# Three low-row matrix products of a fused graph-attention and expert kernel, given 128 rows

## The reference, cut to what matters

```python
x = x + L0_gnn(layernorm(x), adj)   # h = xn @ W; f1 = h @ a1; f2 = h @ a2
                                    # e = leaky_relu(f1[:, None] + f2[None, :], 0.2)
                                    # a = softmax(where(adj > 0, e, -9e15), axis=1); elu(a @ h)
x = x + L0_ffn(layernorm(x))        # 8 experts, top 2, gelu
x = x + L1_gnn(layernorm(x), adj)   # attention whose scores depend on the kind of edge
x = x + L1_ffn(layernorm(x))        # 8 experts, each weighed by one softmax w of shape (1024, 8)
```

## Time and profile before

| | |
|---|---|
| median of 3 executions | 1168.76 us (1166.08 to 1174.06) |
| the profiled execution's own time | 1170.39 us |
| its span, first to last instruction | 1168.6 us |
| mean granted TensorE clock | 0.982 of full speed |
| first attention | 0 to 317 us |
| expert stage | 317 to 489 us |
| second attention | 489 to 813 us |
| last stage | 813 us to the end |

### The profile page before, as it was taken

How to read it: one execution, slowest core, us unless ns; L and a number is a source line. 1 busy time by engine, 2 the same in 40 slices (tenths; PEclk the granted TensorE clock), 3 DMA queues, 4 the chain that set the end, 5 groups by cost and what they waited for, 6 DMA issues and landing times. The chain is left out here.

```text
span 1168.6 us, 18925 instructions
## 1 busy us (share of the span) xinstructions
PE 1100.7 (94%) x5993; PEld 725.8 (62%) x5993; DVE 704.9 (60%) x2210; ACT 744.0 (64%) x1074; POOL 415.9 (36%) x475
## 2 busy tenths in 40 slices
PE   2998899899999999689999999998999999999998
PEld 2554445444477777557777777776546666666667
DVE  4779888888663436287888888864443333333335
ACT  2887777788665554366777777775666556565561
POOL 5327677866765222344556565211000000000000
PEclk9999899899999999899999999999999999999999
DMA  8977557655227665412222222110000000000001
GB/s 260 343 292 265 183 214 285 254 207 210 75 89 245 186 195 168 131 44 84 84 82 82 80 84 80 56 54 1 1 1 10 19 10 10 19 10 19 10 10 37
DMA packets 69142, 131.08 MB, mean 112 GB/s; under 512 B 9918, under 2 KB 30764, under 8 KB 68012
## 3 DMA queue, kind: packets, MB, share of 16 engines
q1 hardware_dynamic: 60268, 111.96, 28.5%
q0 software_dynamic: 8192, 16.79, 4.7%
q10 hardware_dynamic: 576, 1.05, 0.3%
HBM read 77.60 MB, written 52.17 MB: 111 GB/s over the span
## 5 line engine op out<-in xcount | busy, mean ns | idle before, releaser
L2227 PEld LDWEIGHTS eY<-Vo,dGW 128*128 128x128 f32 x1024 | 132.4, 191 | 54.0 <-issue 52.8
L507 POOL DMA_INDIRECT sorted_x<-V,AT_I x128 | 125.9, 984 | 55.8 <-issue 36.2
L2210 PE MATMUL eU<-XTN,V 128*128 128x512 f32 x256 | 132.9, 602 | 2.5 <-PEq L2145 2.5
L2227 PE MATMUL eY<-Vo,dGW 128*128 128x128 f32 x1024 | 134.2, 276 | 0.1
L673 PE MATMUL O<-Y,HS 128*128 128x512 f32 x256 | 134.0, 644 | 0.0
L1863 POOL DMA_INDIRECT W<-sorted_y,ROW_I x96 | 101.0, 1052 | 90.5 <-PE f_T L1923 71.7
L2218 PE MATMUL eU<-H,V 128*128 128x512 f32 x256 | 131.4, 595 | 0.0
L2397 DVE TENSOR_TENSOR dGW<-H,WBC 128x512 f32<-128x512 f32 x80 | 55.2, 691 | 125.2 <-PE eY L2227 125.0
L1942 PEld LDWEIGHTS f_O<-f_XN,f_PT 128*128 128x128 f32 x896 | 107.8, 192 | 25.3 <-issue 20.7
L2306 ACT ACTIVATE H<-eU,bn 128x512 f32<-128x512 f32 x128 | 99.5, 777 | 30.4 <-PE eU L2210 21.3
L1995 ACT COPY f_PT<-f_TP 128x512 f32<-128x512 f32 x128 | 68.7, 589 | 73.2 <-PE f_TP L1932 73.2
(11 more groups left out here) (305 smaller groups left out, 2034.2 us busy)
## 6 DMA issues: line engine op xcount, KB each, us to landing
XTN<-in_adj SPq DMA_DIRECT2D x64, 512.0 KB, 4.7
masks<-NMW SPq DMA_DIRECT2D x8, 2048.0 KB
f_MK<-masks SPq DMA_DIRECT2D x60, 256.0 KB, 2.7
sorted_y<-zero SPq DMA_DIRECT2D x39, 256.0 KB, 10.1
NMW<-sorted_x SPq DMA_DIRECT2D x39, 256.0 KB, 2.7
sorted_y<-NMW SPq DMA_DIRECT2D x39, 256.0 KB, 2.5
X<-in_x SPq DMA_DIRECT2D x8, 512.0 KB, 7.7
out_x<-X SPq DMA_DIRECT2D x16, 256.0 KB, 2.3
```

The source lines that it names most:

```text
L507: g_.indirect_dma_start(sorted_x, bass.IndirectOffsetOnAxis(ap=AT_I[b % 2][:, kt:kt + 1], axis=0), XR[b % 2][:, t * P:(t + 1) * P], None). ...
L2210: pe.matmul(U1[j % 2][:, :], V1[:, e * P:(e + 1) * P], XTN[:, b * N + q * HALF:b * N + (q + 1) * HALF], start=True, stop=True).then_inc(u1 ...
L2227: i = pe.matmul(Y[q][:, t * P:(t + 1) * P], GW[:, j % 2, t * P:(t + 1) * P], Vo[:, e * P:(e + 1) * P], start=(e == 0 and t == 0), stop=(e ...
```

## The change

Every product of few rows becomes one of 128 rows, and its result stays what it was:

- `ones` becomes one 128-row tile of ones for the whole program. POOL's second fill of such a tile goes.
- `F1R` has 128 rows. DVE zeroes it once at the start; the copy still writes three rows.
- `one_row` has 128 rows of 1/128, so the sum over 128 rows is again 1.0.
- `pick` and `WT3` have 128 rows. `pick` is zeroed in all of them, its pattern is written in 24; DVE zeroes `WT3` at the start of the last stage.

```diff
-        ones3 = sb("ones3", [3, P], BF16)
-        pick = sb("pick", [3 * E, E * P], BF16)
+        ones = sb("ones", [P, P], BF16)
+        pick = sb("pick", [P, E * P], BF16)
...
-                v = pick[:, :].rearrange("r (e m) -> r e m", e=E)
+                v = pick[0:3 * E, :].rearrange("r (e m) -> r e m", e=E)
...
-            one_row = tile("one_row", [1, HALF], BF16)
+            one_row = tile("one_row", [P, HALF], BF16)
-            F1R = tile("F1R", [3, 2, N], BF16)
+            F1R = tile("F1R", [P, 2, N], BF16)
-            before, ones = tile("before", [P, P], BF16), tile("ones", [P, P], BF16)
+            before = tile("before", [P, P], BF16)
...
-                op(g_.memset, ones[:, :], 1.0)
...
-                        i = pe.matmul(t[:, h * HALF:(h + 1) * HALF], ones3[:, :], F1R[:, b % 2, h * HALF:(h + 1) * HALF],
+                        i = pe.matmul(t[:, h * HALF:(h + 1) * HALF], ones[:, :], F1R[:, b % 2, h * HALF:(h + 1) * HALF],
...
-                            pe.matmul(O[:, h * HALF:(h + 1) * HALF], ones3[0:1, :], one_row[:, :], start=True, stop=False)
+                            pe.matmul(O[:, h * HALF:(h + 1) * HALF], ones[:, :], one_row[:, :], start=True, stop=False)
...
-                    v.tensor_copy(F1R[:, b % 2, :], F1T[0:3, 0:N]).then_inc(f1r_ready, 1)
+                    v.tensor_copy(F1R[0:3, b % 2, :], F1T[0:3, 0:N]).then_inc(f1r_ready, 1)
...
-                v.memset(one_row[:, :], 1.0)
+                op(v.memset, F1R[:, :, :], 0.0)
+                v.memset(one_row[:, :], 1.0 / P)
...
-            W3, WT3, WT8 = tile("dW3", [P, NT, 3 * E], BF16), tile("dWT3", [3 * E, N], BF16), tile("dWT8", [E, N])
+            W3, WT3, WT8 = tile("dW3", [P, NT, 3 * E], BF16), tile("dWT3", [P, N], BF16), tile("dWT8", [E, N])
...
-                    v.tensor_copy(WT3[:, :], W3T[0:3 * E, 0:N]).then_inc(wt3_ready, 1)
+                    v.tensor_copy(WT3[0:3 * E, :], W3T[0:3 * E, 0:N]).then_inc(wt3_ready, 1)
...
+                op(v.memset, WT3[:, :], 0.0)
                 last_norm()
```

More of the change, by code:

```diff
@@ L172, in _ @@
                 c = Count()
-                for tile, value in ((ident, 0.0), (identb, 0.0), (blockI, 0.0), (pick, 0.0), (ones3, 1.0),
+                for tile, value in ((ident, 0.0), (identb, 0.0), (blockI, 0.0), (pick, 0.0), (ones, 1.0),
                                     (minus_half, -0.5), (eps_all, EPS), (minus1, -1.0),
```

## The result

The changed kernel takes 1158.68 us (median of 4 executions, 1156.27 to 1160.84), the kernel before beside it 1169.72 (4 executions): ratio 0.9884, 95% interval 0.9852 to 0.9917, which is 11.0 us less by the two medians and 13.6 by the ratio. The forecast was 1157.5. A second measurement on another chip gave 0.9882 (0.9839 to 0.9926). The ratios leave out executions that took over 1.5% more than the fastest of their kernel. The profiled execution went from 1170.39 us to 1160.84.

What follows compares the result with a forecast made beforehand. The stage was taken as bound by a chain over PE, ACT, DVE and finally POOL, with nine stretches on PE. Terms -8.4 - 2.3 + 1.0 - 1.5 = -11.2 us took the median from 1168.76 to 1157.5, range 1148 to 1166.

Steps and rivals of the forecast that it cites:

- The reading of distances: PE start to start in the first attention: changing from 128 rows to 3 and back costs 0.19 us a time.
- Rival 3: First attention: the waits are not those of few rows and stay with 128; only the fill is left, 1169.8, chance 0.04.
- L661 and L672, 8.4 us together: First attention, f1 and opening products: full rows save 8.4 us, summed over nine PE stretches.
- the walk: Tracing back from the stage's last product what released each start: a chain over PE, ACT, DVE, POOL with nine PE stretches.
- A quarter arrives, the rest turns into waits: First attention: of PE's 34.6 us saving a quarter arrives, the rest becomes longer waits at L641 and L672.
- The end of the stage: From 278.26 us POOL's root, normalization and scatters run to 311.77; PE's gain after 268.8 is lost in turn(0)'s wait.
- L2265, 2.3 us: Last stage, spread products: each of 8 steps takes 2.16 us instead of 2.44, and all 2.3 us arrive.
- The fill, +1.0: Start of the stage: DVE zeroing F1R takes 0.96 us plus 0.05 of wait, so +1.0 us on the path.
- The clock, -1.5: Half clock on or beside the nine stretches, 27.31 us: bounds 13.7 us either way, taken as -1.5.
- Rival 1: Clock recovers: the 10.24 us half-clock stretch shrinks and one or two others vanish; 5 to 8 us more, 1152, chance 0.27.
- Rival 2: DVE, ACT or POOL take over sooner: half the relief in the stage, -5.5 us, 1163, chance 0.17.
- Rival 4: Slower: PE idles over 2 us at both waits of each sample, the clock falls behind each; +2.3 us, 1171, chance 0.07.

Runs made afterwards that it cites:

- Group 1: Changed kernel with the f1 product on 3 to 128 rows depending on the tile: 1216.31 us in one execution, where the kernel before takes 1222.55.
- group 6: Changed kernel with 3-row f1 products at c = 7, 0 and 1, F1R filled later, attend(61) ahead of turn(0): 1155.88 us, ratio 0.9875.
- group 4: Three kernels, each with one edit on 128 rows against the kernel before: opening 0.9926, f1 product (F1R filled later) 0.9954, spread 1.0009; WT3 zeroed in all.
- opening_alone: Kernel before with only the opening product on 128 rows, and WT3 zeroed: ratio 0.9926 to the kernel before.
- spread_alone: Kernel before with only the last stage's spread product on 128 rows, and WT3 zeroed: ratio 1.0009 to the kernel before.

## Why the prediction was right, and where its steps were off

- **The reading of distances** held at every point: 0.22 us on both sides of L660 (predicted 0.06 behind the last mask product and 0.22 after), 2.15 from opening to `logits` (2.15), 2.15 for a spread step (2.16). Group 1 shows that it is the step to 64 rows or fewer, and not the work, that cost. Rival 3, by which the waits stay, falls.
- **L661 and L672, 8.4 us together.** In the trace the walk was followed closely at first: relu(4) 0.58 earlier (by the steps and the fill 0.72), relu(12) 1.96 (1.96). Between them and relu(36) it isn't level: relu(22) is 4.70 earlier (3.26) and relu(28) 5.00 (4.30), and what came too early is gone at relu(36), 5.09 (5.06). Then more came than it said: relu(46) 10.39 (6.36), of which at relu(52) 9.96 (7.4) are left. Those 2.6 us came where the kernel before had its 10.24 us of half clock; the changed one has a stretch of 3.41 just ahead of this place. At equal clock, openings and `f1` together are worth 11.5 us (4.8 + 6.7), not 8.4. For the openings the term was 7 x 0.48 = 3.4, and 4.8 +- 1.0 came, by a slope that is itself uncertain. For the `f1` product the term was 5.0 and 6.7 came. So this term was too small by some 3 us. The cut of two stretches from 1.72 to 1.3 can hold 0.8 of them. That the walk itself, one chain of one execution, leaves out what a second, nearly equal chain lets through is argued and was not tried.
- **A quarter arrives, the rest turns into waits.** PE's two waits grew from 14.9 to 27.7 us, as said, and full rows at c = 7, 0 and 1, ahead of the wait for `CH`, gave -1.2 +- 1.9 us with the fill, against -7.5 +- 1.3 for the other five tiles, and could be left out in group 6 at no cost that shows. The direction of the walk was right; the share is nearer a third (11.5 of 34.6).
- **The end of the stage.** POOL's chain came as named, but the prediction stopped the account at `turn(0)`, which came 10.0 us earlier, not some 7. PE's longer idle time ahead of it (3.73 us) was followed by half clock in three `attend`s, and 2.0 of 10.0 us went back in the expert stage. No term stood for that.
- **L2265, 2.3 us.** The step is 0.29 shorter, as said, but the stage only 2.0 and 1.8 us in two traces, and 1.4 +- 0.8 over executions. The term counted eight steps; the one with L2272, whose products keep 8 rows, got 0.09 us longer instead, which leaves 1.9. The fill of `WT3`, the rival in group 4, costs 0 to 0.35 us by the last stages of five kernels.
- **The fill, +1.0.** 1.2 us: 0.91 for the fill, and 0.33 ahead of and behind it where 0.05 was taken. Cleared later it doesn't show at the start (first mask product 30.13 us, before 30.03).
- **The clock, -1.5.** 4.8 us less half-clock time by 0.28 is -1.3 us, with an error of 3 us: the value can't be told from none. One of the prediction's own signs of being wrong, stretches of half clock that sum to far from 27 us, did come in the profiled execution: 40.9 us, where all six stretches of before had 30.7. By the slope these 10.2 us are 2.9 us of loss, and over executions there is no more half clock than before (49.8 us, before 54.6). So the term's sign isn't shown either way. Bounding it at 13.7 us was needless width; the spread of executions of the kernel before is 19 us on one chip, and goes with a half-clock time that spans 55 us.
- **Rival 1** (the clock recovers) is what happened in opening_alone, and not in the changed kernel: its stretches of half clock sum to 40.9 us, not less than 30.7. **Rival 2** (other engines take over sooner) put half the relief; POOL does bound the end, but the relief was larger than forecast. **Rival 4** (slower by the clock behind longer waits) may show in small: full rows at c = 7, 0 and 1 on the slowest chip came with 11.8 +- 8.9 us more half clock, 3.3 us by the slope, which is about what those tiles would have gained.

So the mechanism was right, and that the sum met the result to about 1 us by the profiled execution and the medians is in part luck: errors of opposite sign met. The first attention gave some 3 us more than its terms, and the handover took back 2, which had no term.

## What to carry to other kernels

Read the cost of a PE instruction from start to start, and compare what stands on both sides of it: a product of 64 rows or fewer among products of 128 costs 0.19 us more than its duration shows, and zero rows up to 65 or more remove that without more work on PE, if no product of few rows stands beside it. Spend such a gain where no wait follows on the same engine: 16 products right behind a wait gave about all that they saved (3.8 us), and of what 128 products saved (30.7 us) 6.7 arrived. Before comparing kernels by less than 1%, look at the granted clock of each execution. Here taking 0.28 us off for each us of half clock brought the standard deviation of the kernel before from 4.7 to 1.6 us. It makes a comparison sharper, but doesn't show that the clock is the cause.

## What was not expected of the hardware

- The border lies between 64 and 65 rows (0.151 against 0.055 us ahead, 0.318 against 0.220 behind). 33 rows cost what 3 do, and 65 what 128 do but for 0.004 us.
- The same program differs by up to 19 us (1.6%) from execution to execution on one chip, and the differences go with half-clock time (correlation 0.94). Yet two executions on two chips can agree closely: the first attention of spread_alone, where it is the kernel before, has all 64 relus and all six stretches of half clock within 0.04 us of it.
- The chips differ: the kernel before takes 1170 us with 52 to 55 us of half-clock time on three of them, 1222 us with 96 us on the fourth. By the slope, half clock would account for 12 of these 52 us; what makes the rest was not tried.
